# First layer's attention in a two-layer kernel: scores taken twice, float32 values in column strips, division last

## What is computed

```python
qk = (x @ Wqk_w.T + Wqk_b).reshape(b, n, H, E, 2)      # H = 8 heads, E = 8 elements each
q, k = qk[..., 0], qk[..., 1]                          # (b, H, n, E) after the transposes
v = (x @ Wv_w.T + Wv_b).reshape(b, n, H, E)
scores = jnp.einsum('bhqd,bhkd->bhqk', q, k)
attn = jax.nn.softmax(scores, axis=-1) / HEAD_DIM ** 0.5   # HEAD_DIM = 64
out = jnp.einsum('bhsl,bhlv->bhsv', attn, v)
return out @ Wo_w.T + Wo_b
```

## Time and profile before

| | us |
|---|---|
| median of 3 runs | 1701.0 |
| lowest and highest run | 1699.59 and 1701.35 |
| span of the profiled execution | 1699.5 |
| TensorE busy (product records) | 1520.9 |
| VectorE busy | 1081.0 |
| ScalarE busy | 918.1 |
| GpSimd busy | 784.8 |
| first attention, from the first score product to the last value product | 103.4 to 308.2 |
| from there to the last half of `XT` | 308.2 to 347.1 |

### The profile page before, as it was taken

How to read it: one execution, slowest core, us unless ns; L and a number is a source line. 1 busy time by engine, 2 the same in 40 slices (tenths; PEclk the granted TensorE clock), 3 DMA queues, 4 the chain that set the end, 5 groups by cost and what they waited for, 6 DMA issues and landing times. The chain is left out here.

```text
span 1699.5 us, 27381 instructions
## 1 busy us (share of the span) xinstructions
PE 1520.9 (89%) x7804; PEld 1216.0 (72%) x7804; DVE 1081.0 (64%) x1892; ACT 918.1 (54%) x2270; POOL 784.8 (46%) x1102
## 2 busy tenths in 40 slices
PE   4989989659998998999899899899989989989997
PEld 3755555347777877878787787787878778767775
DVE  5558778836666766766676676667666767751222
ACT  3147767236655665655666566566656656642221
POOL 5335545535444544544544454454454445423242
PEclk9979999779999999999999999999999999999998
DMA  4000000401101011010100101001010110122131
GB/s 153 1 1 1 0 1 1 136 22 32 46 14 58 26 31 58 1 57 5 54 32 25 58 26 31 30 29 51 7 58 26 31 39 18 34 96 81 54 124 37
DMA packets 27874, 67.20 MB, mean 40 GB/s; under 512 B 3105, under 2 KB 3233, under 8 KB 27730
## 3 DMA queue, kind: packets, MB, share of 16 engines
q1 hardware_dynamic: 27730, 65.79, 12.4%
HBM read 55.82 MB, written 9.96 MB: 39 GB/s over the span
## 5 line engine op out<-in xcount | busy, mean ns | idle before, releaser
L1085 DVE TENSOR_TENSOR R<-T,R 128x512 fp32r<-128x512 f32 x416 | 284.2, 689 | 98.7 <-ACT R L855 55.1
L569 POOL TENSOR_SCALAR PB<-PB,RI 128x1024 f32<-128x1024 f32 (+7 forms) x320 | 312.0, 975 | 55.6 <-POOL RI L568 46.2
L568 POOL TENSOR_TENSOR RI<-SM,C 128x1 f32<-128x1 f32 x320 | 174.8, 546 | 319.3 <-ACT PB L813 241.2
L1161 DVE CUSTOM_DVE_ANT_0 PB<-S,REL,SLC 128x128 f32<-128x128 f32 (+7 forms) x256 | 207.2, 812 | 100.8 <-PE S L1317 100.5
L813 ACT ACTIVATE PB<-PB,NM 128x128 f32<-128x128 f32 (+7 forms) x256 | 197.7, 772 | 115.7 <-DVE NM L1161 113.7
L855 ACT ACTIVATE R<-T 128x512 fp32r<-128x512 f32 x288 | 169.3, 594 | 135.1 <-PE T L1555 132.8
L1555 PE MATMUL T<-C,PB 128*128 128x128 f32 x1152 | 173.1, 275 | 30.5 <-DVE R L1085 13.3
L1315 PE MATMUL S<-R 128*128 128x512 f32 (+2 forms) x488 | 183.3, 376 | 9.6 <-DVE NM L1161 4.6
L1555 PEld LDWEIGHTS T<-C,PB 128*128 128x128 f32 x1152 | 134.1, 140 | 60.7 <-DVE R L1085 24.5
L1317 PE MATMUL S<-R 128*128 128x512 f32 (+2 forms) x488 | 174.6, 358 | 0.0
L1316 PE MATMUL S<-R 128*128 128x512 f32 (+2 forms) x488 | 173.8, 356 | 0.0
(11 more groups left out here) (159 smaller groups left out, 3641.6 us busy)
## 6 DMA issues: line engine op xcount, KB each, us to landing
RAW<-w SPq DMA_DIRECT2D x36, 384.0 KB, 3.6
PB<-dequantised SPq DMA_DIRECT2D x20, 512.0 KB, 3.7
RAW<-w SPq DMA_DIRECT2D x38, 256.0 KB, 2.6
DQ<-codes SPq DMA_DIRECT2D x16, 352.0 KB, 3.4
DQ<-absmax SPq DMA_DIRECT2D x16, 352.0 KB, 3.0
dequantised<-DQ SPq DMA_DIRECT2D x16, 352.0 KB, 2.3
PB<-x SPq DMA_DIRECT2D x16, 256.0 KB, 3.0
x_scratch<-PB SPq DMA_DIRECT2D x8, 256.0 KB, 3.2
```

The costliest lines, as they stand in the source:

```text
L568: ch.link(e.tensor_tensor(RI[:, k:k + 1], SM[:, k:k + 1], C[:, C_EXP + 5:C_EXP + 6], ALU.pow))
L569: e.tensor_scalar(PB[:, m % 2, a, 0:L], PB[:, m % 2, a, 0:L], RI[:, k:k + 1], scale, ALU.mult, ALU.mult).then_inc(probs_ready, 1)
L1085: e.tensor_tensor(r(o + 512, 512), bank[:, :], rf(o, 512), ALU.subtract).then_inc(t_free, 1)
L1161: e.tensor_tensor_reduce(out=PB[:, m % 2, a, 0:L], in0=bank[:, 0:L], in1=REL[:, TOK - L:TOK], scale=SLC[:, a:a + 1], scalar=3.0e38, op0=AL ...
```

## The change

**Shape of the work.** A unit `u` (4 of them) is a block of four heads and half of the queries, 512. A step is a unit and a key block `kb`; there are 32.

**Maxima first.** `max0` makes the same score products as before (16 tiles of 128 queries by 1024 keys per unit, now going round the four heads' strips), and VectorE takes the negated row maximum, but nothing else reads these scores. `shift` splits the 16 maxima of a row into a high and a low part on VectorE, `shift0` transposes them on TensorE, `shift_rows` copies them to `R`.

**Scores again, keys on partitions.** `keys0` makes, for each head, 128 keys by 512 queries in one of three banks `SB` (the two `T` banks and `WB`), and a second product of 32 contraction rows adds the shift, with ones as the stationary operand. ScalarE takes the exponential straight from PSUM into float32 `PT0`, 128x512, with no bias and no row sum. The transposes, the two halves and GpSimd's division are gone.

**Values.** `values0` is one float32 product per head, with no halves: 32 stationary columns (8 values, a column of ones that gives the row sum, zeros) and 512 moving columns, written to the head's 32 partitions of `VB`. ScalarE copies `VB` to `SUMS` once per unit.

**Division last.** For each token tile the sums are transposed (`OS`), VectorE inverts 8 row sums and scales the values twice, into 128 columns (`ON`); they are transposed (`OH`), split by ScalarE and VectorE, and two fp32r products follow where `mm3` stood. The stages of a tile are spread over 13 steps, `OUT_STEPS`, that were 11.

**Smaller moves.** GpSimd clears `VF` at the very start and no longer pads values. SyncE loads x anew after the last but one group of value products, where it was before the last pass. ScalarE no longer copies blocks; the maxima of unit u+1 stand between the steps of unit u by `MAX_AT`.

```diff
-SCORE_AT = {0: 0, 1: 1, 2: 2, 4: 3}
-EXP_AT = {0: 0, 2: 1, 3: 2, 5: 3}
+MAX_AT = {0: (0, 1, 2), 1: (3, 4, 5), 2: (6, 7, 8), 3: (9, 10, 11), 4: (12, 13), 5: (14, 15)}
...
-        TMP = [PBF[:, (8 + t) * D:(9 + t) * D] for t in range(6)]
+        TMP = [PBF[:, (8 + t) * D:(9 + t) * D] for t in range(4)]
+        PT0 = [PBF[:, k * HEADS * D:(k + 1) * HEADS * D] for k in range(3)]
+        VF = PBF[:, 6144:8192].rearrange("p (b h e) -> p b h e", b=NT, h=H0)
+        SUMS = [CMP[:, 0, :], CMP[:, 1, :], LA[:, 1024:1536], LA[:, 0:512]]
+        SHF = RT[:, :, :].rearrange("p a n -> p (a n)")
...
+        SB = [T[0], T[1], WB]
...
-            sp.wait_ge(t_full, T_ATT + (2 * H0 - 1) * NT)
+            sp.wait_ge(pv_done, PV_BASE - 1)
...
+            e.memset(VF[:, :, :, :], 0.0).then_inc(vf_clear, 1)
+            hold(pool, vf_clear, 1, p_passed)
+            e.memset(VF[:, :, :, E0:E0 + 1], 1.0).then_inc(vf_clear, 1)
...
-            ch.link(e.memset(rf(VPAD_AT[0], 4096), 0.0))
...
-            for n in range(2 * H0):
-                for a in range(4):
-                    divide(n, a, TOK, n * 4 + a + 1, 1.0 / math.sqrt(H0 * E0))
-                if n == 0:
-                    pad_values(6, 2)
...
+            hold(pool, t_free, T_QK + 8, p_passed)
+            e.memset(rf(ONES0, P), 1.0).then_inc(vf_clear, 1)
...
-                e.activation(PB[:, n % 2, a, :], S[u % 2][:, :], ACT.Exp, bias=NM[:, k:k + 1],
-                             accum_out=SM[:, k:k + 1]).then_inc(exp_done, 1)
...
+            def sums0(u):
+                act.wait_ge(pv_done, (u + 1) * NT)
+                if u == 3:
+
+                    act.wait_ge(t_full, T_HW + NT)
+                e.activation(SUMS[u], VB[:, :], ACT.Copy).then_inc(sums_ready, 1)
+
+            for u in range(UNITS):
                 for kb in range(NT):
...
-                    e.activation(r(PT + c % 3 * 1024, 512), T[k % 2][:, :], ACT.Copy).then_inc(t_act, 1)
...
+                    x = u * NT + kb
+                    if x >= 3:
+
+                        act.wait_ge(pv_done, x - 2)
+                    if x == 2:
+
+                        act.wait_ge(gate_done, NT)
+                    for h in range(HEADS):
+                        c = x * HEADS + h
+                        act.wait_ge(st_full, c + 1)
+                        e.activation(PT0[x % 3][:, h * D:(h + 1) * D], SB[c % 3][:, :], ACT.Exp).then_inc(st_exp, 1)
+                    if u and kb == 0:
+                        sums0(u - 1)
+            sums0(UNITS - 1)
...
+            def max0(u, x):
+                v = u * SLOTS0 + x
+                dve.wait_ge(s_full, S_ATT + v + 1)
+                e.tensor_reduce(MX[:, x:x + 1], S[v % 2][:, :], AX.X, ALU.max, negate=True).then_inc(max_done, 1)
+
+            def shift(u):
+
+                dve.wait_ge(max_done, u * SLOTS0 + 16)
+                rows_ = SHF.rearrange("p (b h n) -> p b h n", b=4, h=HEADS)
+                mx = MX[:, :].rearrange("p (b h) -> p b h", b=4)
+                hi = r(SHIFT + 1280, 16)
+                ch.link(e.tensor_copy(hi, MX[:, :]))
+                hi = hi.bitcast(F32).rearrange("p (b h) -> p b h", b=4)
+                ch.done(e.tensor_copy(rows_[:, :, :, 0], hi))
+                ch.settle()
+                e.tensor_tensor(rows_[:, :, :, 1], mx, hi, ALU.subtract).then_inc(shift_ready, 1)
+
+            def shift_rows(u):
+
+                v = u * SLOTS0 + 16
+                dve.wait_ge(s_full, S_ATT + v + 1)
+                e.tensor_copy(r(SHIFT + u % 2 * 512, 512), S[v % 2][:, 0:512]).then_inc(max_done, 1)
 
...
-                    low_pt(T_ATT + c + 1, c, T[(T_ATT + c) % 2], c)
...
+                    k = T_AT["OS", s]
+                    dve.wait_ge(t_act, k + 1)
+                    dve.wait_ge(t_full, k + 1)
+                    sums = T[k % 2][:, 0:256].rearrange("p (h e) -> p h e", h=H0)
+                    ch.link(e.reciprocal(RS[:, s % 2, :], sums[:, :, E0]))
...
+                    inv = RS[:, s % 2, :].unsqueeze(2).to_broadcast([P, H0, E0])
+                    e.scalar_tensor_tensor(on[:, :, 0, :], sums[:, :, 0:E0], -1.0 / math.sqrt(H0 * E0), inv,
+                                           ALU.mult, ALU.mult).then_inc(on_ready, 1)
+                    e.scalar_tensor_tensor(on[:, :, 1, :], sums[:, :, 0:E0], -1.0 / math.sqrt(H0 * E0), inv,
+                                           ALU.mult, ALU.mult).then_inc(t_free, 1)
...
+                    o = OT + t % 2 * 256
+                    e.scalar_tensor_tensor(r(o + P, P), rf(o, P), C[:, C_MASK + 3:C_MASK + 4], T[k % 2][:, 0:P],
+                                           ALU.mult, ALU.subtract).then_inc(t_free, 1)
...
+                    e.tensor_tensor(tmp, WB[:, :], ROWS[:, R_BO:R_BO + D], ALU.add).then_inc(w_free, 1)
+                    dve.wait_ge(w_free, t + 1)
+                    e.scalar_tensor_tensor(tmp, tmp, 0.5, G[:, t * D:(t + 1) * D], ALU.mult, ALU.mult)\
+                        .then_inc(tmp_ready, 1)
...
+            def max0(u, x):
+                qb, h = x // HEADS, x % HEADS
+                v = u * SLOTS0 + x
+                if v >= 2:
+                    pe.wait_ge(max_done, v - 1)
...
+                    last = e.matmul(S[v % 2][:, c * 512:(c + 1) * 512], R[b, qc:qc + P], R[b, kc:kc + 512],
+                                    start=True, stop=True)
                 last.then_inc(s_full, 1)
...
-                e.matmul(VB[:, :], v, r(o, 512), start=first, stop=False)
-                e.matmul(VB[:, :], v, r(o + 512, 512), start=False, stop=end).then_inc(pv_done, 1)
...
+            def keys0(u, kb):
+                if kb == 0:
+                    pe.wait_ge(max_done, (u + 1) * SLOTS0)
+                for h in range(HEADS):
+                    c = (u * NT + kb) * HEADS + h
+                    if c >= 3:
+                        pe.wait_ge(st_exp, c - 2)
+                    b, blk, tok = rows0(u, h)
+                    kc, qc = KS + blk + kb * P, QS + blk + tok
+                    e.matmul(SB[c % 3][:, :], R[b, kc:kc + P], R[b, qc:qc + 512], start=True, stop=False)
+                    e.matmul(SB[c % 3][:, :], R[b, ONES0:ONES0 + P], R[b, SHIFT + u % 2 * 512:SHIFT + u % 2 * 512 + 512],
+                             start=False, stop=True).then_inc(st_full, 1)
+
+            def values0(u, kb):
+                x = u * NT + kb
+                pe.wait_ge(st_exp, (x + 1) * HEADS)
+                if u and kb == 0:
+                    pe.wait_ge(sums_ready, u)
+                for h in range(HEADS):
+                    last = e.matmul(VB[h * 32:(h + 1) * 32, :], VF[:, kb, u % 2 * HEADS + h, :],
+                                    PT0[x % 3][:, h * D:(h + 1) * D], start=kb == 0, stop=kb == NT - 1)
+                last.then_inc(pv_done, 1)
...
-                    for a in range(4):
-                        last = e.transpose(T[k % 2][:, a * P:(a + 1) * P], PB[:, n % 2, a, kb * P:(kb + 1) * P], IDENT)
-                    last.then_inc(t_full, 1)
-                    if c >= 2:
-                        values0(c - 2)
...
+                    keys0(u, kb)
+                    if u + 1 < UNITS:
+                        for x in MAX_AT.get(kb, ()):
+                            max0(u + 1, x)
+                        if kb == 6:
+                            shift0(u + 1)
+                    if u or kb:
+                        y = u * NT + kb - 1
+                        values0(y // NT, y % NT)
...
-                mm3(WB[:, :], r(o, P), r(o + 512, P), r(WO0_H, D), r(WO0_L, D), True, True).then_inc(w_full, 1)
...
+                        e.matmul(WB[:, :], r(o, P), r(WO0_H, D), start=True, stop=False)
+                        e.matmul(WB[:, :], r(o, P), r(WO0_L, D), start=False, stop=True).then_inc(w_full, 1)
```

290 lines of the change are left out of this document (145 added, 145 removed).

## The result

The changed kernel takes 1737.5 us (median of 4 runs, 1734.6 to 1746.5) where the kernel before takes 1701.1 (4 runs beside it): ratio 1.0222, 95% interval 1.0205 to 1.024. The prediction was 1663, faster; it is slower by 36.4 us. Its profiled execution spans 1736.2 us.

The account below looks back on a forecast made before the run. Before, a ring of waits with no engine full alone; after the change TensorE decides. Loop -48.5 us and the stretch after it +10 give -38.5 from 1701.0: 1662.5, say 1663, range 1645 to 1750.

Parts of the forecast that it names:

- rival 3: TensorE's clock stays at 1.2 GHz through the loop, all starts double, loop ends at 353, total 1756 us; chance 4%.
- The value group: Four float32 value products of a step, side by side in four strips: 1.1 us with changes of kind.
- Rival 1: A step's four float32 value products run one after another, 3.65 us a group, total 1743 us; chance 30%.
- The key chunks: Second score products of a step: 0.35 us a chunk, neighbours partly overlapping, 1.5 a step with the change of kind.
- a step without maxima: Loop step with only key chunks and values: 2.6 us, ScalarE's 2.44 hidden under it.
- Steps with maxima: Loop steps also holding the next unit's pairs: 5.33 us with three, 3.74 with two; the shift's step 3.45.
- the sum of the loop: First key product at 127.9, then 104.6 + 20.8 + 4 + 2.4 us, last value product at 259.7.
- the 4 us between units: In the loop, the shift's copy and the copy of the sums stand in the way, 1.4 x 3 = 4 us.
- After the loop: Output stretch grows by +10 us (+3.0 before the first tile, +7.2 on VectorE), from +6 to +14.
- Start: First unit's bare maxima, 19.5 us from 106.1, then 2.3: keys at 127.9; GpSimd's early clear +0.2 at most.
- The second layer is untouched: The part behind the first layer was taken as unchanged, with no term in the sum.
- The 0.15 us from a pair's end to its maximum: In the loop, VectorE's start after a score pair's end, counted in the third pair's wait within 2.73 us.

Follow-up runs that it names:

- a_vmid: a_order with 185 instructions without work added on TensorE, the values issued ahead of the fourth key chunk; 1690.3 us, ratio 0.9915.
- a_serial: a_order with 185 instructions without work, all heads' value products in one column strip for seven of eight key chunks; 1716.8 us, one run.
- a_ser2: a_pad with all heads' value products in one column strip for seven of eight key chunks; total not given, loop clock 0.87, one run.
- a_order: The changed kernel with the fourth key chunk behind the first two maximum pairs and the third pair behind the values; 1672.4 us, ratio 0.9838.
- a_vfill2: a_vmid with the first product of the fourth key chunk (32 rows) issued twice more in each step; 1725.2 us.
- a_pad: The changed kernel with 185 instructions without work in TensorE's queue, spread over the first eight transposes; 1700.9 us, ratio 1.0032.
- b_pad: The kernel before with 71 instructions without work added on TensorE ahead of the loop; 1719.5 us, ratio 1.0118.

## Why the prediction was wrong, point by point

- **The step that failed is rival 3, given 4%.** Its argument against was one sentence, "TensorE's terms fill over 80% of each step". They did (157.7 of 193.9 us), and the clock was 0.52 all the same, where the sum took every product at the high level. The profile had no row with products of 32 rows beside four strips for a stretch of any length, so I judged a new mix by an argument about time filled, where a_vmid (92% filled, 0.54) against a_serial (89%, 0.93) shows that this does not carry. The rival's price was too high: its loop was to take 225 us (127.9 to 353, all starts doubled) and took 193.9, since TensorE's waits for VectorE and ScalarE do not grow with the level (a step of 4.97 against 3.13). That its total of 1756 lies only 18 us above the measured one is in part luck, as it had nothing for the second layer's 21.
- **The value group, on which I thought all hung, was right.** 1.1 us forecast, 1.06 by record and 0.99 to the next keys. One strip after another was to cost 2.55 more (3.65 less 1.1), and a_serial measured 2.55. Four in a row are 3.62 by record, 0.90 for one float32 product, which is the split price. Here the Trainium skill (FP8 and Floating Point Precision, on precision modes: four passes) agrees. For four row strips the Trainium skill gives 3.07x (TensorE: Matmul & The Clock Gate, part 3, packing); these column strips brought 3.62 / 1.06 = 3.4. Rival 1, given 30%, did not happen.
- **The key chunks were mis-sized, through a wait that I had not placed.** Each was to cost 0.35, 1.5 a step with the change of kind; the four cost 2.13. Three start together, but the fourth waits 0.73 for the first exponential, behind which the values stand in order. So a step without maxima is 3.13 and not 2.6 at the high level. There are 11 of them, 6 us in the loop.
- **Steps with maxima were priced right for the high level, so the sum of the loop held there.** In the order as given, a_ser2 has such steps at the high level; less the 2.56 us by which its value group is longer they are 5.22 with three pairs (forecast 5.33), 3.13 and 3.58 with two (3.74) and 3.71 with the shift (3.45). The one with three, from the first key product to the next step's:

```profile
182.94 0.50 PE L1488 MATMUL WB<-R 32*128 32x512 f32 x1
...
186.51 0.73 PE L1467 MATMUL S<-R 32*128 32x512 f32 x2 [1.35 <-DVE MX L1102]
187.17 3.62 PE L1499 MATMUL VB<-PB 128*32 128x512 f32 x8
190.72 0.50 PE L1488 MATMUL T<-R 32*128 32x512 f32 x2
```

An estimate from these: three units of 34.4 us, eight steps of 3.13 and 1 at the end give a loop of about 130 us, where 131.8 was forecast. So about all of the 62 us are the clock, and the wait of the fourth chunk is made up for by other terms, among them the 4 us between units, of which the rows show little. At the low level the changed kernel's steps with maxima take 5.0 to 8.4 us. In a_order one with three pairs takes 4.2 at the high level, so its order alone is worth 1 us there.

- **After the loop:** +10 forecast, +6.6 measured (45.4 against 38.8, from the earlier trace rows), near the end of +6 that I named for small operations that fall into waits. VectorE's first output operation comes 3.1 us behind the start of the last copy of `VB` (317.32 to 320.45), where 4.3 was forecast.
- **Start:** 4.5 us earlier than forecast: the first score product 5.5 earlier, maxima and shift 1.0 longer (25.5 for 24.5). I priced what the change adds on GpSimd and not what it takes from beside VectorE: 4.1 us for the clear.
- **"The second layer is untouched"** put at nothing a term of 21 us. No instruction of it changed, but its place in TensorE's instruction stream did.
- **Small slips in the working.** By its own sums (10.4, 10 and 10 us in a pass of 12) each engine's work is within 17% of the pass, not 15%. The 0.15 us from a pair's end to its maximum (154.23 to 154.38) is no hand-over, since VectorE was at the operation of 153.77 until then. Neither moves the result.
- The range, up to 1750, held the time, but it reached so far for rival 1's sake, which did not happen; that was luck. The forecast's direction was wrong.

## What to carry to other kernels

A change that makes TensorE's products narrow and parallel should be priced at both clock levels before anything else is summed, and the time that TensorE's records fill is no argument for the high one. Where a long TensorE loop follows, look at the instruction queue's transfers in both profiles: a shift of the loop's start by instructions without work gave back 1.2% of this kernel and took 1.1% of the one before. And list an ordered step bank by bank: the wait of the fourth chunk for one of three banks, unseen here, was worth 0.5 us in each step without maxima, and moving this chunk behind two maximum pairs and the third pair behind the values, with the padding, turned +2.2% into -3.1%.

## What the runs showed of the hardware that I had not expected

- The clock stayed at its low level through all but 7 of 194 us in which TensorE's records fill 81%, and in a_vfill2 through all of 201 us with 91%; the same loop with two added products a step over 128 rows ran at 0.88.
- The executions of one kernel can differ in their clock: ten runs of a_pad lie between 1694.9 and 1718.2 us, of a_vmid between 1675.7 and 1698.8, the longer ones at the lower mean clock (0.902 for 1717.3 us, 0.920 for 1694.9; 0.903 for 1698.8, 0.928 for 1675.7), where the kernel before varies by 0.2%.
- The instruction queue that follows TensorE's code brings about 16 KB a transfer (0.46 MB in 28). The second layer's loop went without any transfer in some positions (the kernel before, a_pad) and took 8 to 10 in each of five passes in others (45 in the changed kernel, 44 in b_pad). The cost shows as one wait a pass, of 3 to 5 us, and is 21 us in all.
- A GpSimd clear of 128x4096 (3.5 us) beside a VectorE cast of 128x512 made the cast 3.10 us in place of 0.43; the cast ended 0.3 us behind the clear.
